# Constant matmuls on TensorE ahead of, behind and between the first steps of an attention and expert kernel, and q's first operands loaded ahead of k's

## The reference, cut to what matters

```python
B, T, _ = x.shape                                   # 8, 512, 128
q = apply_rope((x @ Wq).reshape(B, T, 2 * H, HD))   # H = 16, HD = 4
k = apply_rope((x @ Wk).reshape(B, T, 2 * KVH, HD)) # KVH = 8
v = (x @ Wv).reshape(B, T, KVH, 2, HD)
attn1 = causal_attn(q1, k1, vcat, scale)
attn2 = causal_attn(q2, k2, vcat, scale)
attn = attn1 - lambda_full * attn2                  # then RMS norm, @ Wo
x = layernorm(x + attn_out)
# experts: softmax router, argmax expert e of 8
y = silu(a) * g @ w2[e],  a, g = split(x @ w1[e])
x = layernorm(x + y * max_prob)
```

## Time and profile before

| | |
|---|---|
| median of 3 runs | 682.83 us (674.66 to 687.29) |
| the profiled execution | 680.83 us, its span 679.0 us |
| TensorE busy | 602.4 us, 89% of the span |
| VectorE busy | 517.0 us, 76% |
| ScalarE busy | 426.6 us, 63% |
| mean granted TensorE clock | 0.908 |

### The profile page before, as it was taken

How to read it: one execution, slowest core, us unless ns; L and a number is a source line. 1 busy time by engine, 2 the same in 40 slices (tenths; PEclk the granted TensorE clock), 3 DMA queues, 4 the chain that set the end, 5 groups by cost and what they waited for, 6 DMA issues and landing times.

```text
span 679.0 us, 29739 instructions
## 1 busy us (share of the span) xinstructions
PE 602.4 (89%) x12409; PEld 333.0 (49%) x12409; DVE 517.0 (76%) x1285; ACT 426.6 (63%) x896; POOL 312.3 (46%) x509
## 2 busy tenths in 40 slices
PE   3299999999988998999899999989999898699982
PEld 1145344444533543444344444434444488599972
DVE  2277799998996997799698879967964488756662
ACT  1103688888976886787688778766876435234441
POOL 3222033462865366375535646520534205636674
PEclk9655699999998999899999999986987699899997
DMA  3513313313411331242124114210106443535580
GB/s 122 167 44 100 89 32 90 103 32 79 111 47 43 78 110 37 57 111 75 45 77 109 33 49 111 71 39 25 35 8 218 141 157 126 197 128 192 191 263 21
DMA packets 44486, 63.86 MB, mean 94 GB/s; under 512 B 13440, under 2 KB 35584, under 8 KB 44080
## 3 DMA queue, kind: packets, MB, share of 16 engines
q1 hardware_dynamic: 38816, 54.38, 27.5%
q0 software_dynamic: 2272, 4.69, 1.9%
q10 hardware_dynamic: 3264, 2.89, 1.4%
HBM read 43.88 MB, written 21.65 MB: 97 GB/s over the span
## 4 chain that ended last, share of the span: by engine, by line
PE 60%; DVE 25%; issue 7%; DMA 2%; ACT 2%; POOL 2%; SPq 0%; ACTq 0%; POOLq 0%; DVEq 0%
PE bank L712 16%; DVE mr L1327 15%; PE bank L646 9%; PE bank L628 9%; PE bank L838 7%; PE bank L851 3%; PE bank L720 3%; PE bank L749 3%; PE bank L665 2%; PE bank L723 2%; PE bank L759 1%; DVE rl L1313 1%; DMA rope<-in_c_rope 1%; PE bank L730 1%; PE bank L753 1%
## 5 line engine op out<-in xcount | busy, mean ns | idle before, releaser
L1327 DVE TENSOR_REDUCE mr<-bank 128x8 f32<-128x512 f32 x576 | 369.4, 682 | 75.0 <-PE bank L646 57.6
L909 ACT ACTIVATE work<-bank 128x512 f32<-128x512 f32 x576 | 314.9, 600 | 98.7 <-PE bank L665 79.6
L712 PE MATMUL bank<-work,v_aug 128*32 128x512 f32 (+7 forms) x2048 | 187.1, 443 | 1.6 <-issue 1.6
L646 PE MATMUL bank<-kd,qd 24*64 24x192 bf16 (+7 forms) x2048 | 179.1, 303 | 5.2 <-issue 5.2
L628 PEld LDWEIGHTS bank<-bits 32*64 32x64 bf16 x4608 | 80.5, 107 | 193.5 <-DVE mr L1327 134.2
L665 PE MATMUL bank<-qd,kd 27*64 27x512 bf16 (+7 forms) x2048 | 170.8, 297 | 1.9 <-issue 1.9
L628 PE MATMUL bank<-bits 32*64 32x64 bf16 (+2 forms) x4608 | 137.1, 216 | 30.6 <-DVE mr L1327 14.2
L1086 POOL CAST msplit<-mt 128x32 bf16<-128x32 f32 x32 | 6.8, 211 | 166.5 <-DVE mt L1337 166.4
L838 PE MATMUL bank<-xr,wbuf 128*128 128x256 f32 (+1 forms) x368 | 76.7, 364 | 5.0 <-DVE xr L1582 4.4
L712 PEld LDWEIGHTS bank<-work,v_aug 128*32 128x32 f32 x2048 | 47.7, 112 | 56.5 <-issue 28.4
L646 PEld LDWEIGHTS bank<-kd,qd 24*64 24x64 bf16 x2048 | 70.6, 114 | 9.4 <-issue 9.4
(11 more groups left out here) (182 smaller groups left out, 628.0 us busy)
## 6 DMA issues: line engine op xcount, KB each, us to landing
wbuf<-in_w SPq DMA_DIRECT2D x23, 768.0 KB
qk_parts<-parts SPq DMA_DIRECT2D x90, 128.0 KB, 2.7
kd<-qk_parts SPq DMA_DIRECT2D x64, 96.0 KB
qd<-qk_parts SPq DMA_DIRECT2D x64, 96.0 KB
x_sorted<-in_c_pad SPq DMA_DIRECT2D x9, 390.0 KB, 4.3
xr<-x_sorted SPq DMA_DIRECT2D x16, 130.0 KB
xt_s<-in_xT SPq DMA_DIRECT2D x8, 256.0 KB, 3.9
xn<-in_x SPq DMA_DIRECT2D x7, 256.0 KB
```

What stands on the lines that cost most here:

```text
L646: m = pe.matmul(bk[L * c:L * c + L, cols], qd[lo:lo + KROWS, s % 2, second, c, L * n:L * n + L], kd[lo:lo + KROWS, s % 2, second, c, 0:key ...
L712: m = pe.matmul(pv_b[32 * t:32 * t + 32, L * kb:T], v_aug[:, vb, kv + v, kb, :], cols, start=kb == 0, stop=True, skip_group_check=True)
L909: nc.scalar.activation(prob[:, pos, r, :], st_b[no % ST_RING][:, :], ACT.Exp, scale=HD ** -0.5).then_inc(s_sfree, 1)
L1327: V.tensor_reduce(mr[:, s % 2, u % 2, i, i:i + NB], nat_b[no % NAT_RING][:, :].rearrange("p (n t) -> p n t", t=L), AX.X, ALU.max)\
```

## The change

On TensorE three kinds of filler are added; each multiplies constants into pv_b, and nobody reads the result. `busy_early(20)`: 20 bfloat16 matmuls of 128x128 by 512 columns on kd as soon as kd is set, ahead of the projections. `busy(22)`: 22 float32 matmuls of 128x128 by 512 columns on wq_s, behind the projection of v and ahead of the waits for phase 0. `busy(1 + t % 2)`: one or two of the same float32 matmuls in each slot of phases 0 and 1, 13 in a phase.

On the queues, the writes of k's parts 1 and 2 (three DMAs) move from ScalarE's queue to SyncE's, behind q's writes. ScalarE computes part 1 of k ahead of its three DMAs of part 0. For pair 0 SyncE loads qd first and then kd, and the load of the next batch's x (xt_s) comes behind both instead of ahead.

```diff
-                for a, dst, done in ((1, kd, s_kd), (0, qd, s_qd)):
+                for a, dst, done in ((0, qd, s_qd), (1, kd, s_kd))[::-1 if s else 1]:
                     wait(sp, s_written[a], STORED * (b + 1))
                     load_rows(sp, dst, s, a, done[q])
...
             write_parts(sp, 0, 0)
+            for term, of in TERMS_OF[1]:
+                if of:
+                    wait(sp, s_split[1], PART_DONE[of])
+                    sp.dma_start(qk_parts[0, 1, :, :, term].rearrange("f x d w t -> (f x) (d w) t"), parts[:, 1, of, :])\
+                        .then_inc(s_written[1], 16)
+            sp.wait_ge(s_kminus, 1)
+            operands(0)
             sp.wait_ge(s_first, 3)
             sp.dma_start(xt_s[:, :], xT[:, 1]).then_inc(s_xt, 16)
-            sp.wait_ge(s_kminus, 1)
-            operands(0)
...
+            def busy_early(n):
+
+                for _ in range(n):
+                    pe.matmul(pv_b[:, :], kd[:, 0, 0, 0, 0:P], kd[:, 1, 0, 0, :], start=True, stop=True)
+
+            def busy(n):
+
+                for _ in range(n):
+                    pe.matmul(pv_b[:, :], wq_s[:, 0, :], wq_s[:, :, :].rearrange("p c m -> p (c m)"),
+                              start=True, stop=True)
+
+            pe.wait_ge(s_kminus, 1)
+            busy_early(20)
             pe.wait_ge(s_wq, 16)
...
             project_v(banks[4]).then_inc(s_first, 1)
+            busy(22)
             pe.wait_ge(s_bits, 16)
...
                     for u in (2 * t, 2 * t + 1):
                         scores(g, u)
+                    if g < LAG:
+                        busy(1 + t % 2)
                     for name, n in uses(g, t):
                         use(name, n)
...
             part(1, 0)
+            part(1, 1)
             for term, of in TERMS_OF[1]:
-                if term == 1:
-                    part(1, 1)
-                wait(act, s_split[1], PART_DONE[of])
-                act.dma_start(qk_parts[0, 1, :, :, term].rearrange("f x d w t -> (f x) (d w) t"), parts[:, 1, of, :])\
-                    .then_inc(s_written[1], 16)
+                if not of:
+                    act.dma_start(qk_parts[0, 1, :, :, term].rearrange("f x d w t -> (f x) (d w) t"), parts[:, 1, of, :])\
+                        .then_inc(s_written[1], 16)
```

## The result

The changed kernel takes 689.54 us in the median of 4 runs (685.32 to 690.98); the kernel before, 678.75 of 4 (673.59 to 687.29). The ratio is 1.0187, 95% interval 1.0134 to 1.0240: the change made the kernel slower, by some 12.7 us if one goes by the ratio (the two medians lie 10.8 apart). Whether it is more or less than 2% the interval leaves open. The time lies in the predicted range, but the kernel before turned out 4 us faster than the three runs shown ahead, so the step is larger than the 7 that were forecast.

What follows compares the result with a forecast made beforehand. It took a wait on the HBM chain until 29.50, VectorE's pace in phases 0 and 1, and half-speed TensorE in phase 2 as bounds. 11.4 late less 5.8 gives 5.6, plus 1.4 makes 7: 682.83 + 7 = 690, range 682 to 698.

Steps and rivals of the forecast that it cites:

- the 7 that were forecast: Whole kernel: the change makes it 7 us slower, 682.83 to 690 in the median.
- The queue path: Start, DMA queues: qd and kd both landed by 25.0, 4.5 us earlier than 29.50.
- v's end: Start, projections on TensorE: with the clock up at 10.6, q, k and v done at 15.2 instead of 17.6.
- 22 fillers: Behind v's projection: 0.86 us each, 18.9 us in all, TensorE not free until 34.1.
- Phases 0 and 1: Slots of phases 0 and 1: TensorE is the bound, 1.5 and 2.4 us a slot, phases of 18.3 and 18.5.
- I expect one such fall: Phase 2, before its first pv: the clock falls once, costing at most 1.7 us, some 1.4.
- rival A: Phase 2: the clock falls before the first pv and stays down to the phase's end; 12 us slower, 695; 28%.
- phase 3's turn: Turn of the row maxima of phase 3 on VectorE, expected near 87.
- The 5.8 us that a warm clock was to give back: Phase 2: the low clock costs 5.8 us, 18.48 from turn to turn against 12.7 at full clock.
- Rival B: All float32 fillers: each costs 0.43 us, not 0.86, and they are hidden; 668 us; 8%.
- C: All fillers: they don't lift the clock at all, phase 2 begins at 117, 740 us; 3%.
- Rival D: Slots of phases 0 and 1: fillers overlap better with scores and VectorE, 16 us a phase, 685 us; 9%.

Runs made afterwards that it cites:

- x2: The changed kernel with 11 float32 fillers behind v in place of 22; 681.27 us, ratio 1.0110 to the kernel before.
- x6: Changed kernel with 11 fillers behind v, three bfloat16 fillers per slot in phases 0, 1 and slots 0 to 2 of phase 2; 640.94 us, ratio 0.9867.
- x8: x5 without the 20 early fillers; 669.64 us, ratio 0.9885 to the kernel before.
- x5: Changed kernel with 11 fillers behind v and three bfloat16 fillers per slot of phases 0 and 1 in place of float32 ones; 663.59 us, ratio 0.9841.
- x1: The changed kernel without the 26 fillers in the slots of phases 0 and 1; 680.99 us, ratio 1.0072 to the kernel before.
- x3: The changed kernel with all three kinds of filler taken out, only the queue moves left; 671.12 us, ratio 0.9949 to the kernel before.
- x4: The changed kernel with 11 fillers behind v and none in the slots; 675.90 us, ratio 0.9987 to the kernel before.
- x11: x5 with one bfloat16 filler a slot in place of three; 643.27 us on the faster chip, ratio 0.9918 to the kernel before.
- x9_bf_slots_none_behind: x5 without the 11 fillers behind v, early and slot fillers kept; 679.10 us, no ratio given.
- x10: x5 with the queues of the kernel before; 651.34 us on the faster chip, ratio 1.0007 to the kernel before.
- x12: The same kernel as x5, timed once more on the faster chip; 645.10 us, ratio 0.9932 to the kernel before.

## Why the prediction was right, and where not

**The start** was right. The queue path was forecast to give operands at 25.0; where eleven fillers didn't hide it, phase 0 waited for them until 25.2 (x2) to 26.7 (x6). v's end was put at 15.2 (the terms given, 10.6 + 3.5 + 0.9, make 15.0) and came at 15.8, since the rope table landed 0.64 later. 22 fillers took 19.1 for 18.9 forecast, 0.868 each for 0.86, and phase 0 began at 34.9 for 34.1.

**Phases 0 and 1** were right in kind and a little small: TensorE is the bound, 1.47 and 2.33 a slot for 1.5 and 2.4, 18.7 and 19.2 a phase for 18.3 and 18.5. Phase 2 began at 72.98 where 70.9 was forecast, 14.7 later than before.

**Phase 2** is the step that failed: "I expect one such fall", at some 1.4 us. The place was right, and so was the price of a fall as short as that: x8, with one of 3.4 us, took 14.0 from turn to turn for the 12.6 of x5. The length wasn't. The clock was at 0.50 from 76 to 100, phase 2 took 18.99 for the 12.7 forecast and the next took 13.79 where 12.12 was to be had; phase 3's turn, put near 87, came at 95.1. That is rival A, put at 28%. The forecast took the length from one fall far into the run (it did end at 373.7, as the prediction says, though the earlier trace rows stops there), and the table above has falls of 3.4 to 27.3 us at this place. So the slots without pv are the cause of the fall, and how long it lasted, the forecast's 3.4 us or rival A's phase, was up to the execution as far as these traces show.

The 5.8 us that a warm clock was to give back in phase 2 came from one execution too. In x1, x3 and x4, whose phase 2 also began at 0.50, the clock came back some 5 us behind the turn and phase 2 took 14.5 to 14.8, not 18.5. By these, some 2 us were to be had.

With the fall, the changed kernel stands 15.8 us late at phase 4's turn of the maxima (108.88 against 93.07), and at the end of the span 10.2 (689.2 against 679.0). The 5.6 between came back behind phase 4, where both kernels are alike: before took 585.9 us from there at a mean clock of 0.94, after 580.3 at 0.95, with 68 and 55 us at 0.50. No cause in the change was looked for, and falls of the clock differ like this from execution to execution.

**The total** was right partly by luck: the step against before is 12.7 us (9.1 to 16.3 by the interval), rival A's 12, not the forecast's 7, while the level of before was 4 us lower than the runs shown. Rival B, fillers of 0.43, is out (0.868 measured), and so is C: the fillers lift the clock and hold it from 8 to 76. Rival D's 16 a phase didn't happen.

What the change was worth by parts: queues and early fillers some 4 us at the start (x2's 25.2, or x5's 26.0, against 29.6), about half each by x3 and x8; fillers behind v beyond the eleventh, minus 9; slots with float32 fillers, minus 9 against the same phases at half speed; and a clock that was lost anyway. The version with 11 behind v and three bfloat16 fillers a slot beats the kernel before, by 1.6% on one chip and 0.7% on another, and so the changed kernel as well. How much of that needs all three fillers isn't shown: with one a slot (x11) the gain was 0.8% beside those 0.7%.

## What to carry to other kernels

A filler is work on an engine that runs in order: count its matmuls by the price of their type and size, and place no more than reaches the moment at which real work is ready. 1.2 us of float32 filler beside 1.2 us of another engine's pace made TensorE the bound; 0.65 of bfloat16 held the clock as well and cost 0.02 in a slot without a projection. Look where the fillers end as much as where they stand: in six traces of seven the clock was lost in the first thin stretch behind the last one. And read the length of such a loss from several executions: one trace gave 3.4 us, another 27.3.

## What the runs showed of the hardware

A wholly busy TensorE didn't always get its clock back. In x9_bf_slots_none_behind it was 12.40 busy of 12.40 at 0.50, with fillers of the full array among the scores that held 1.00 in x5_bf_slots. There, holding the clock was cheaper than regaining it: the turn of phase 2 came 5.9 us later than in x5.

A wait of 2.84 us (x10) and one of 2.72 ahead of the projections (x1) were each followed by half speed. At the latter place waits of 1.59 (the changed kernel), 2.05 (x12) and 2.30 (x4) were not. Each is one execution.

The float32 fillers took 0.434 a record on 512 columns, bfloat16 ones of the same size some 0.22. And one chip ran every version some 27 us faster than the others. The same kernel took 19.69 from the turn of phase 12 to the next on one chip (x5) and 14.00 on that one (x12), and every fourth phase from there on shows such a difference. Why stays open.
